# Four fused layers on one Trainium2 core: unread matmuls in front of TensorE's waits, and other stage orders

## What is computed

```python
x = L0(ctx, x, mask, ...)   # 16 heads: x asks, the keys and values are of ctx and x; rmsnorm; gelu MLP of 1024
x = L1(x, ctx, ...)         # token mixing, then a recurrence over the 64 tokens: s = a + w * s
                            # group norm, gate, out projection, channel mixing
x = L2(x, ctx, ...)         # one head: softmax((x Wq)(ctx Wk)^T / 16) (ctx Wv) Wo^T, times alpha, added
x = L3(x, ctx, amask, ...)  # 32 query heads on 8 key heads, mask, layer norm with gamma and beta
```

## Time and profile before

| | |
|---|---|
| median of 3 runs | 1574.29 us (1573.39 to 1576.73) |
| the profiled execution, its own time | 1566.94 us |
| its span, first to last instruction | 1565.1 us |
| mean granted PE clock | 0.957 |
| busy: PE, PEld | 1407.5 us (90%), 1084.5 us (69%) |
| busy: DVE, ACT, POOL | 1063.2 us (68%), 622.6 us (40%), 618.7 us (40%) |

### The profile page before, as it was taken

One profiled execution on the slowest core, in us unless ns is written; L12 is line 12 of the kernel. 1 busy time (PEld: TensorE's weight loads), 2 busy tenths in 40 slices (PEclk: granted clock), 3 DMA queues, 4 the chain that ended last, 5 costly groups with the idle time before them and its releaser, 6 DMA issues.

```text
span 1565.1 us, 34489 instructions
## 1 busy us (share of the span) xinstructions
PE 1407.5 (90%) x14312; PEld 1084.5 (69%) x14312; DVE 1063.2 (68%) x2073; ACT 622.6 (40%) x1351; POOL 618.7 (40%) x604
## 2 busy tenths in 40 slices
...
PEclk9899999999999999999999999999989999999776
...
DMA packets 65787, 70.40 MB, mean 45 GB/s; under 512 B 19808, under 2 KB 54752, under 8 KB 65248
## 3 DMA queue, kind: packets, MB, share of 16 engines
...
## 4 chain that ended last, share of the span: by engine, by line
PE 78%; DVE 10%; ACT 6%; issue 3%; POOL 2%; DMA 1%; POOLq 0%; SPq 0%; DVEq 0%; ACTq 0%
PE pw L454 18%; PE pw L432 14%; PE pw L640 7%; PE pw L634 7%; PE pw L438 4%; PE pw L490 4%; PE pw L576 4%; PE pw L585 4%; PE pw L538 3%; PE pw L443 2%; ACT ptA L857 2%; PE pw L755 2%; DVE ab L1293 2%; DVE big L1272 2%; ACT ptC L859 1%
## 5 line engine op out<-in xcount | busy, mean ns | idle before, releaser
L1293 DVE TENSOR_TENSOR_SCAN ab<-pw,ab 128x256 f32<-128x256 f32 x256 | 159.1, 672 | 73.6 <-ACT ab L967 48.4
L1046 POOL TENSOR_TENSOR ab<-big,kvrg 128x504 f32<-128x504 f32 x128 | 161.1, 1259 | 91.1 <-PE pw L454 58.0
L1082 POOL TENSOR_TENSOR ab<-ab,kvrg 128x512 f32<-128x512 f32 x128 | 162.2, 1273 | 4.7 <-DVE ab L1293 4.6
L1031 POOL TENSOR_TENSOR vtmp_A<-mv_A,eps 128x2 f32<-128x2 f32 x16 | 3.1, 194 | 372.2 <-DVE mv_A L1154 372.2
L1069 POOL TENSOR_TENSOR big<-big,xaB 128x512 f32<-128x512 f32 x80 | 92.5, 1174 | 101.6 <-DVE big L1272 101.5
L432 PE MATMUL pw<-big,wb 128*128 128x256 f32 x512 | 130.9, 406 | 0.0
L634 PE MATMUL pw<-tA,wb 128*128 128x256 f32 x512 | 121.1, 391 | 1.5 <-DVE tA L1237 1.5
L1272 DVE SCALAR_TENSOR_TENSOR big<-pw,wa,sxB 128x256 f32<-128x256 f32 x160 | 67.1, 477 | 77.4 <-PE pw L538 77.3
L432 PEld LDWEIGHTS pw<-big,wb 128*128 128x128 f32 x512 | 99.0, 201 | 26.1 <-issue 9.4
L640 PE MATMUL pw<-wb,ptA 128*128 128x256 f32 x512 | 116.7, 382 | 0.0
L634 PEld LDWEIGHTS pw<-tA,wb 128*128 128x128 f32 x512 | 98.2, 195 | 20.9 <-issue 5.4
...
## 6 DMA issues: line engine op xcount, KB each, us to landing
big<-kvrg SPq DMA_DIRECT2D x256, 128.0 KB, 3.9
...
```

What stands on the lines that cost most here:

```text
L1046: G.tensor_tensor(ab[i % 4][:, :, :, 1:S], vx[i % 3].rearrange("p j (b s) -> p j b s", b=NB)[:, :, :, 0:S - 1], k, ALU.mult).then_inc(kv_p ...
L1082: G.tensor_tensor(ab[i % 4][:, :, :, :], st[i % 2][:, :, :, :], r, ALU.mult).then_inc(pd_ok, 1)
L1293: last = V.tensor_tensor_scan(st[i % 2][:, j, :, :].rearrange("p b s -> p (b s)"), kn(b5)[:, i // 4, :], ab[i % 4][:, j, :, :].rearrange(" ...
```

## The change

It does two things. First, `warm(k, n)` lets PE issue n matmuls of 128x256 (the identity times a piece of the weight `q0`) into the bank of ring slot k, after the wait that the next real writer of that slot has anyway. Nobody reads them: the next real writer of the slot overwrites them. `WARM` says before which stages of the PE order they stand and how many, 116 at 32 places, all in tiles 0, 1, 14 and 15. `NEXT` gives the slot that is next at each stage.

Second, all strings of `FLOW` are others, for all five engines, in the head, the round and the tail.

```diff
 FLOW = {
     "PE": (
...
-        "ABAABBCBBABBBBBABBBACCCBBABBCBBBBACBACBCACBBCBCAACCBBBBBABBACACAAABBCACACACCBCCBC",
...
+        "ABABABABBBCBBBBABBBCCBACBBBBBACBABCABCBCACCCAACABBBBCBBBACACAAABCACBABCBBACCBCBCC",
...
 SLOT, TURN = numbers()
+
+
+def upcoming():
+
+    out, k = {}, 0
+    for name, i, t in sequence("PE"):
+        k = SLOT.get((name, i, t), k)
+        out[name, i, t] = k
+        if (name, i, t) in SLOT:
+            k += USES[name]
+    return out
+
+
+NEXT = upcoming()
+
+
+WARM = {
+    ("max0", 1, 0): 9, ("turn0", 0, TILES - 2): 1, ("exp0", 1, 0): 3, ("exp0", 1, TILES - 2): 3,
+    ("value0", 0, 0): 4, ("out0", 0, 1): 2, ("norm0", 0, TILES - 1): 3, ("zturn", 0, 0): 10,
+    ("zturn", 0, TILES - 1): 4, ("up", 1, 1): 1, ("xturn", 0, 0): 2, ("ruk", 0, 0): 3,
+    ("cv", 0, TILES - 1): 1, ("scan", 1, 0): 4, ("scan", 3, TILES - 2): 1, ("scan", 5, 0): 10,
+    ("sum", 3, TILES - 2): 1, ("oturn", 1, TILES - 1): 8, ("gnorm", 2, TILES - 1): 2, ("gturn", 0, 1): 1,
+    ("norm2", 0, 0): 1, ("cturn", 0, TILES - 1): 2, ("x2turn", 0, TILES - 2): 4, ("x2turn", 0, TILES - 1): 3,
+    ("v3", 0, TILES - 1): 2, ("x3turn", 0, 0): 3, ("max1", 0, TILES - 1): 1, ("exp1", 0, TILES - 1): 7,
+    ("exp1", 1, TILES - 2): 3, ("exp1", 1, TILES - 1): 3, ("norm3", 0, 0): 6, ("norm3", 0, TILES - 2): 8,
+}
+
+
+def warm_count(name, i, t):
+
+    return WARM.get((name, i, t if t in (0, 1, TILES - 2, TILES - 1) else "round"), 0)
...
             mm = nc.tensor.matmul
+
+            def warm(k, n):
+
+                if k >= FIRST_FREE:
+                    pe.wait_ge(*spare(k))
+                for _ in range(n):
+                    mm(bank(k)[:, 0:C], ident, w("q0", 0), start=True, stop=True)
...
             def stage(name, i, t):
+                if warm_count(name, i, t):
+                    warm(NEXT[name, i, t], warm_count(name, i, t))
```

More of the change, by code:

```diff
@@ L81 @@
     "PE": (
[L82 to L87 removed]
+        ("AAAAAAAAAAAAAAAAAAAAAABABBBABABBBBBABBBABABBBBABBBAAABABBBABAABAABBABBAAABBBBABBBAABCBABCBCBBBBABBBB"
+         "BCCABACBBBABBBCCBCACCABBCCACBAABBCABBBABBBAAACACBACBCCBBCCAC"),
@@ L88 @@
+        "ABABABABBBCBBBBABBBCCBACBBBBBACBABCABCBCACCCAACABBBBCBBBACACAAABCACBABCBBACCBCBCC",
+        ("BAAABABBCBBBBBBCBABBACBBBCBBBACCABBCAABABACCBABCBBCCCBBBACBABBCABAACBABCACAABCBCAABBABBCBCCBBBABBBBC"
+         "BABACCBCBBCBBCACBBCBBCCCCACABBBCBABCABBBAABAABCAAAAABCBBCBCCBCBBCBBBBCBBCBBBBCCBCBBBCBCCBCCCBBCBBCCB"
+         "BCBBCBCBCBBCBBCBCBCCCCCCCCCCCCCCBCCCCCCCCCCCC"),
     ),
     "DVE": (
-        ("AAAAAAAAAAAAAAAAAAAAABAABBBBBBABBBABABBBBAABBBABAAABABABABBABBBBABABBBABBABAABBBABAACBCBACCBBBBAABBB"
-         "BABABBCBBBBBCACCBCBACBCCBBBBBCBAACABAAACBCAABBCBCAACCBCACCBB"),
@@ L92 @@
[L92 to L95, removed]
+        ("AAAAAAAAAAAAAAAAAAAAAABBBABBBAABBBBBABBBBBBBBBBAAAAAAAABBBBAABAABABBBBBBBAABABBBAACBBABCBBBBCABACBBB"
+         "BBCABBBBCBCCBBACABCCACCBBABACBABABBABCABBBBACAACAACACBBCBCCC"),
```

40 lines of the change are left out of this document (22 added, 18 removed).

## The result

The changed kernel takes 1599.94 us (median of 4 runs, 1597.75 to 1601.41), the kernel before 1574.24 us in runs of the same session. The ratio is 1.0158, 95% interval 1.0142 to 1.0174: 25 us **slower**. The forecast was 1561 us, with a range up to 1578 us. It was wrong in sign, and the result lies outside the range.

A forecast was written before the change was run, and what follows sets the result against it. TensorE was taken to bound the kernel by its work, waits and half clock. Head -6 + 2, tail -9.5, rounds +5.5 - 5 summed to -13 us: 1561 us off the median of 1574.3 us, range 1545 to 1578 us.

The forecast's parts named there:

- part 2: The new orders of the eleven repeated rounds: +5.5 us from shifted waits, -5 us from the clock.
- The other moved stages: turn0, sum 2, GpSimd's scans and additions, SP's copies: no wait of PE there, other engines slack; zero, +-3 us.
- four moves in the round: On PE gturn behind exp1 1, mix1 before v0, max0 0 swapped with cturn; on VectorE gturn's products before value1's reciprocal.
- Part 1, the clock's gain: Unread matmuls in head and tail hold PE's clock up: 6 of 8.9 us and 9.5 of 17.2 us recovered.
- Part 1, the overrun: Unread matmuls that outlast the waits they fill: +2 us in the head, none in the tail.
- the 13.5 us booked: Net gain of the unread matmuls: head -6 + 2, tail -9.5 us.
- Part 2, the chain of a round: VectorE's later reciprocal moves mix2's stall to mix1 and k0: +1.4 - 0.55 - 0.35 = +0.5 us a round.
- Part 2, the rounds' clock: Waits at mix2 no longer close together, so a quarter of the rounds' 19 us clock loss returns: -5 us.
- The rival that all of it recovers: The rounds' clock recovers too, another -14 us: 1547 us; chance 0.22.
- Slower by VectorE's chain: In each round the chain from gturn through value1 to xturn delays PE and drops the clock: 1595 us; chance 0.16.
- That the unread matmuls do not hold the clock: In head and tail the clock falls anyway: about 1575 us, 1582 us at worst; chance 0.14.
- The Trainium skill's rule of the prediction: Ramp penalty under 1% of a typical kernel's span, at most 15.7 us here; its place moves from run to run.

The follow-up runs named there:

- the fitted version: Kernel before, old orders, plus unread matmuls: two before each mix2 wait of tiles 2 to 13, 28 in tile 0, 37 in tiles 14 and 15: 1535.92 us.

## Why the prediction was wrong

**The step that failed** is the last sentence of part 2: "The other moved stages ... zero, with +-3 us for all." The new tail costs 25 us and the new head 10 us. The reason given, that those stages stand where PE had no wait and other engines have slack, says nothing of an order as a whole: the tail of before kept PE idle for 7.3 of 175 us, and the new order makes PE wait a dozen times and more for 0.3 to 1.4 us, and for 3.65 us at `zturn`, with one store 13 us late. The figure beside it does not hold either: in the rounds VectorE is busy 73% of the time, ScalarE and GpSimd 42%, which is no 67 to 75% idle. Which moves make the waits of head and tail stays open but for the store. I costed four moves in the round and left two thirds of the new strings, those paid once, unread; paid once, they were the larger part.

**Part 1, the clock's gain: right in size on the orders that its rows show.** Booked were 6 us in the head and 9.5 us in the tail. On the old orders the clock gave back 6.6 and 11.1 us, on the new ones 12.0 and 14.8 us: without unread matmuls those lose more to the clock (0.93 and 0.87 against 0.95 and 0.89).

**Part 1, the overrun: mis-sized on the rows it was worked out from.** Booked were 2 us and none; on the old orders, whose waits those rows show, it was 11.2 and 7.4 us. On the new orders it was 7.4 and 2.9 us. The net there, 15 us by the ratios and 16.5 us by the stretches, met the 13.5 us booked since both terms had grown: luck. I had compared sums (21.1 us against 31.3 us idle), but only those behind a wait of their own length are free.

**Part 2, the chain of a round: its waits right, short in size.** `k0` 0.72 us (0.9 forecast), `mix1` 1.06 us (1.1), none at `mix2` 0, the second `mix2` wait 0.85 us (1.16 - 0.35 = 0.81), the reciprocal 1.0 us later (1.15). The round at full clock grew by 0.9 us and not 0.5 us; a wait that the sum did not have is that of 0.37 us at the last `mix2` group. The late reciprocal explains the wait of `k0` alone: with `gturn` back it was gone, and that of `mix1` stayed at 1.06 us.

**Part 2, the rounds' clock: not settled, and small.** Of the stake a quarter, 5 us, was to come back. At full clock eleven rounds would last 987.3 us in the old order and 997.0 us in the new. In the profiles of before and after they lasted 1003.6 and 1014.1 us: 16.3 and 17.1 us lost to the clock, nothing back. But the nine profiles of the old round without fills lost 15 to 27 us, 21 us in the mean, and the three with the new one 15.5 to 17 us. So 4 us came back in the mean, none in the pair, within the spread of single profiles. The rival that all of it recovers is excluded: with waits of 0.72, 1.06 and 0.85 us at `k0`, `mix1` and `mix2` the new rounds still lost 16 us. Covering the waits gave nearly the whole, but that was done on the old round only.

**The rivals.** Slower by VectorE's chain gave 1595 us, 5 us from the result, but for another reason: that chain is worth 0.46 us a round, 5 us in all. A near number, and no support for the mechanism. That the unread matmuls do not hold the clock is excluded by 0.99 in the head. The Trainium skill's rule of the prediction ("TensorE: Matmul & The Clock Gate", "What's actually happening") has two halves. The first, a ramp penalty under 1% of a typical kernel's span, does not bound the losses of this kernel, which are falls of the clock all along it: covering the waits gave 2.1%. The second, that the place moves from run to run, agrees: in the kernel before and in the one with the new tail alone, which are the same up to the `k0` of tile 14, the falls lie in different rounds (full clock in the 2nd, 5th, 7th and 10th round there, in the 3rd, 5th, 8th and 10th here). Its consequence as a rival, that a count fitted to one run need not fit the next, was not seen: the four runs of the fitted version lie within 2.4 us.
